# Four passes over an 8192x8192 matrix: the first pass with seven products per block from block row 4 on, one group and one join per row

## Chip, cores and metric

The kernel runs on one core of one Trainium2 chip. The metric is the device time of one execution in microseconds (us). The kernel before takes 1793.39 us, the median of three runs (1792.01 to 1795.44).

## What is computed

The matrix `adj` (8192x8192, float32) multiplies a thin matrix of 64 features four times, each time with the result of the time before:

```python
h = relu(layernorm(x))
T1 = adj @ h
T2 = 2 * (adj @ T1) - h
T3 = 2 * (adj @ T2) - T1
x = x + h @ w[0] + T1 @ w[1] + T2 @ w[2] + T3 @ w[3] + bias0
h = relu(layernorm(x))
p = tanh(norm(h)) * h / (norm(h) + 1e-8)        # norm clipped to [0, 10]
s = adj @ p
x = x + (arctanh(norm(s)) * s / (norm(s) + 1e-8)) @ kernel + bias1   # norm clipped to 0.999
```

## The kernel before

The matrix is cut into 16x16 blocks of 512x512 (1 MB, numbers `(r, c)`: r is the rows of the result, c the rows of the thin matrix that it multiplies). A block holds four chunks of 128. Blocks come from HBM through `ring`, 13 slots of one block each, all issued by SyncE in one fixed order; a load waits on `visits_done` until the last visit of the block that had its slot is over. `nodes[:, chunk, A or B, :]` holds the thin matrices: A is h, later T2; B is T1, later p. The level of a product is 1 (from h), 2 (from T1), 3 (from T2), 4 (from p).

`work_order()` writes out one list of steps, and every engine walks through that list. The steps that TensorE runs ("visits") are:

- `FRESH(r, c)`: level 1 alone from a loaded block, into `row_bank` (L627). Eight matmuls in the hardware, of 128x512.
- `BOTH(r, c)`: two levels from one load. In the first sweep levels 1 and 2 for a block left of the diagonal, into one of three `work_bank` in turn (L638 and L640), which VectorE adds to `partial[:, r, :]` after each block (L1036; the first is a copy, L1033).
- `AGAIN(r, c, level)`: one more level from a block that is in the ring already (L757), added by VectorE (L1050 to L1056). In the first sweep this is level 2 of the diagonal block.
- `OWN`: level 3 alone.
- `H_TURN`, `H_TERM`: small products with h in row 0 (L794, L807).

After the last block of a row comes `SUM` (VectorE L1079 and ScalarE L874 put the row into `acc`), then `TURN` on TensorE (L840, into `turned`), then VectorE writes the features of the next level into `nodes` (L1155, L1157, L1197). Only then may a visit use them (`s_known`).

There are three sweeps over the matrix. The first gives level 1, and level 2 for blocks on and left of the diagonal; the second, backwards, gives level 2 right of the diagonal together with level 3; the third the rest of level 3 with level 4. In the first sweep before the change `rows` (FRESH, row by row) and `columns` (one AGAIN, then BOTH down a column) are two queues, and the loop takes one of each in turn, a BOTH as soon as level 2 of its column is known. It ends with the corner of rows and columns 13 to 15.

In the second and third sweep some rows are "fast" (`is_fast`): TensorE makes seven half-size products per block in place of eight (L689). For this VectorE first forms three differences of block parts ("mixing", L1021, L1025, L1027, into `ring` slots that are given up, double-buffered by `mix_of`), two visits ahead of the visit, and GpSimd forms four sums of features (L582 to L587) once per column. At the end of a fast row ScalarE copies and exchanges halves of the two banks (L884, L887), and VectorE joins them (`JOIN`, L1116 to L1135). While rows are fast, 5 of the 13 slots (`GIVEN_UP`) hold sums and mixed blocks, and 8 are left for loads. `fast` pairs of banks alternate, so that one row is joined while the next one runs. In the second sweep column 13 (`PLAIN_COLUMN`) is done without the seven products, and its block is not mixed (L709).

```python
    while rows or columns:
        if columns and (next_is_known(columns) or not rows):
            v = columns.pop(0)
            visit(*v)
            if v[0] == "AGAIN":
                continue
        if rows:
            visit(*rows.pop(0))
```

Of the kernel before, what the change touches and what calls it, by code (L numbers as in the profile page):

```python
# [7 lines left out]
FAST_BELOW, FAST_FROM, LATE_FROM = 10, 6, 8  # L8
# [3 lines left out]
def work_order():  # L12
# [49 lines left out]

    def both_columns(row):
        if sweep[0] == 0:
            return range(min(row, HIGH))
# [4 lines left out]
    def row_complete(row, level):  # L70
        both = all((sweep[0], "BOTH", row, c) in done for c in both_columns(row))
        if level == 1:
            return both and all((0, "FRESH", row, c) in done for c in range(min(row, HIGH), NB))
        if level == 2 and row >= HIGH:
            return all((0, "AGAIN", row, c) in done for c in range(HIGH, NB))
# [4 lines left out]
    def visit(kind, row, col, *level):  # L80
        steps.append((kind, row, col) + level)
        done.add((sweep[0], kind, row, col))
        if kind == "AGAIN":
# [8 lines left out]
    def next_is_known(queue):  # L92
        kind, row, col, *level = queue[0]
        if kind == "AGAIN":
            summed = ("JOIN" if row >= FAST_FROM else "SUM", row, 3)
# [3 lines left out]


# [14 lines left out]
    while rows or columns:  # L115
        if columns and (next_is_known(columns) or not rows):
            v = columns.pop(0)
            visit(*v)
            if v[0] == "AGAIN":
                continue  # L120
        if rows:
            visit(*rows.pop(0))
        if left:
            steps.append(left.pop(0))
    for c in range(HIGH, NB):
        for r in (range(HIGH, NB) if c < NB - 1 else reversed(range(HIGH, NB))):
            visit("AGAIN", r, c, 2)
# [49 lines left out]
def with_sums(steps):  # L177

    out, waiting, corner = [], [], True
    last_corner = [s for s in steps if s[0] == "AGAIN" and s[3] == 3][-1]  # L180
    for s in steps:
        out.append(s)
        if s == ("SUM", 0, 2):
            corner = True
        if s[0] == "TURN" and s[2] == 2 and s[1] >= LOW:
            waiting.append(("SUMS", s[1], 3))
        if s[0] == "EXPAND" and s[1] < NB - 2:
            waiting.append(("SUMS", s[1], 4))
        if s in (last_corner, ("AGAIN", LOW, LOW, 4)):
            corner = False  # L190
        if not corner:
# [7 lines left out]
def is_fast(row, level):  # L199

    return level == 2 and row < FAST_BELOW or level == 3 and row >= FAST_FROM
# [36 lines left out]
def chebyshev_hyperbolic_kernel(nc, x, adj_blocks, cheb_weight, cheb_bias, hyp_kernel, hyp_bias, out):  # L238
# [18 lines left out]
    bank_no, bank_users = {}, []  # L257
# [15 lines left out]
    fast = [i for i in in_order if steps[i][0] == "BOTH" and phase_of[i] > 0 and is_fast(steps[i][1], phase_of[i] + 1)]  # L273
# [3 lines left out]
    fast_rows = [s[1:] for s in steps if s[0] == "SUM" and is_fast(*s[1:])]  # L277
    fast_second = sum(level == 2 for r, level in fast_rows)
# [8 lines left out]
    last_visit_of = [0] * len(first_step_of)  # L287
    for i, s in enumerate(steps):
# [981 lines left out]
```

How the kernel before makes its waits and increments, by code:

```python
        @block.sync  # L535
        def _(sp):
            def load_x(g):
                rows = slice(H_GROUPS[g][0] * C, (H_GROUPS[g][-1] + 1) * C)
                sp.dma_start(resid[:, rows, :], x[:, rows, :]).then_inc(s_x[g], 16)
            for n in range(loads):
                r, c = steps[first_step_of[n]][1:3]
                if n == 0:
                    load_x(0)
                    load_x(1)
                if n + 2 < len(H_GROUPS):
                    load_x(n + 2)
                if freed_by[n]:
                    sp.wait_ge(s_visit, freed_by[n])
                sp.dma_start(ring[:, slot_of[n], :, :], adj_blocks[(r * NB + c) * P:(r * NB + c + 1) * P, :, :])\
                    .then_inc(s_landed[slot_of[n]], 16)
            for s in steps:
                if s[0] == "RESULT":
                    for r in s[1:]:
                        if r in by_pool:
                            sp.wait_ge(s_pooled, by_pool.index(r) + 1)
                        else:
                            sp.wait_ge(s_result, by_vector.index(r) + 1)
                        sp.dma_start(out[:, chunks(r), :], resid[:, chunks(r), :]).then_inc(s_out, 16)
            sp.wait_ge(s_out, NB * 16)
# [1 line left out]
        @block.gpsimd  # L562
# [1 line left out]
            nc.gpsimd.memset(ident[:, :], 0.0)  # L564
            nc.gpsimd.memset(w_h[:, :, :], 0.0).then_inc(s_zeroed, 1)
            pool.wait_ge(s_zeroed, 1)
            nc.gpsimd.affine_select(out=ident[:, :], in_=ident[:, :], compare_op=ALU.not_equal, fill=1.0,
```

## Time and profile before

| | |
|---|---|
| median of the runs | 1793.39 us |
| profiled execution, its own time | 1793.74 us |
| its span, first to last instruction | 1791.8 us |
| granted TensorE clock | 0.997 |
| TensorE busy | 1756.5 us (98%) |
| VectorE busy | 962.0 us (54%) |
| loads of blocks | 626, 660.64 MB on the load queue |
| HBM read | 658.74 MB |
| start of the second sweep's first BOTH | 726.75 us |

The span leaves out what lies before the first and behind the last instruction (1.9 us here). Busy shares are means over three sweeps, which differ; the rows below are therefore taken by stretch. A line like L689 stands for one source line of the kernel before.

### The profile page before, as it was taken

What the parts mean: (1) busy time and instruction counts of PE and PEld (TensorE: products, weight loads), DVE (VectorE), ACT (ScalarE), POOL (GpSimd) and SP (SyncE); (2) the same over time, 40 slices, a digit from 0 to 9 for tenths busy, and PEclk for the clock granted to TensorE, in tenths of its full rate; (3) what the DMA queues carried; (4) which work ended last, traced back from release to release, by engine and by line L of the source; (5) the groups of instructions that cost most, each with busy time, mean ns of one, the idle gap of its engine ahead of it and who ended that gap; (6) DMA issues with size and microseconds to landing.
All of it is one profiled execution on the core that took longest, in us unless ns stands there. A gap on an engine that the chain in (4) does not pass through costs nothing.

```text
span 1791.8 us, 44489 instructions
## 1 busy us (share of the span) xinstructions
PE 1756.5 (98%) x20100; PEld 889.1 (50%) x20100; DVE 962.0 (54%) x1540; ACT 177.1 (10%) x333; POOL 126.4 (7%) x173
## 2 busy tenths in 40 slices
PE   7999999999999999999999999999999999999997
PEld 4544444444444444456666654345554454544443
DVE  7211211112111223268888886558788877876856
ACT  1000000000000000011011001311111111010014
POOL 0000000000000000221100100211001100110003
PEclk9999999999999999999999999999999999999998
DMA  9999999999999994689999988599999999999995
GB/s 370 421 422 420 422 421 413 397 397 389 377 388 383 388 361 185 251 312 330 330 339 341 334 321 339 223 348 384 417 419 419 420 419 411 419 410 418 419 420 217
DMA packets 94923, 663.72 MB, mean 370 GB/s; under 512 B 11408, under 2 KB 13712, under 8 KB 14608
## 3 DMA queue, kind: packets, MB, share of 16 engines
q1 hardware_dynamic: 93744, 660.64, 93.0%
q8 instruction: 160, 2.62, 0.6%
q10 hardware_dynamic: 992, 0.23, 0.1%
q14 instruction: 27, 0.22, 0.0%
HBM read 658.74 MB, written 2.10 MB: 369 GB/s over the span
## 4 chain that ended last, share of the span: by engine, by line
PE 87%; DVE 6%; DMA 5%; issue 1%; SPq 1%; ACT 0%; DVEq 0%
PE work_bank L638 19%; PE work_bank L757 14%; PE own_bank L689 13%; PE row_bank L689 13%; PE row_bank L627 13%; DMA ring<-adj_blocks 5%; PE row_bank L734 4%; PE work_bank L640 3%; PE turned L840 2%; DVE ring L1021 1%; PE own_bank L782 1%; PE work_bank L709 1%; PE work_bank L782 1%; DVE ring L1025 1%; DVE partial L1056 1%
## 5 line engine op out<-in xcount | busy, mean ns | idle before, releaser
L638 PE MATMUL work_bank<-ring,nodes 128*64 128x512 f32 x936 | 420.8, 592 | 0.0
L640 PE MATMUL work_bank<-ring,nodes 128*64 128x512 f32 x936 | 420.8, 592 | 0.0
L757 PE MATMUL work_bank<-ring,nodes 128*32 128x512 f32 (+1 forms) x2600 | 327.9, 593 | 8.8 <-DVE nodes L1197 4.8
L1036 DVE TENSOR_TENSOR partial<-partial,work_bank 128x512 f32<-128x512 f32 x102 | 70.1, 687 | 405.0 <-PE work_bank L640 405.0
L627 PE MATMUL row_bank<-ring,nodes 128*64 128x512 f32 x1112 | 269.8, 595 | 8.1 <-DMA ring<-adj_blocks 8.1
L689 PE MATMUL row_bank<-ring 128*32 128x256 f32 x3104 | 267.7, 379 | 0.2
L689 PE MATMUL own_bank<-ring 128*32 128x256 f32 x3104 | 267.4, 379 | 0.1
L1021 DVE TENSOR_TENSOR ring<-ring 128x1024 f32<-128x1024 f32 x194 | 238.8, 1231 | 36.8 <-PE own_bank L689 18.0
L689 PE MATMUL own_bank<-ring,nodes 128*32 128x256 f32 x2328 | 237.5, 379 | 1.3 <-DVE ring L1021 1.3
L689 PE MATMUL row_bank<-ring,nodes 128*32 128x256 f32 x2328 | 235.8, 379 | 0.7 <-DVE ring L1021 0.6
L638 PEld LDWEIGHTS work_bank<-ring,nodes 128*64 128x64 f32 x936 | 127.9, 137 | 218.0 <-issue 218.0
L757 PEld LDWEIGHTS work_bank<-ring,nodes 128*32 128x32 f32 (+1 forms) x2600 | 100.1, 112 | 160.7 <-issue 140.4
L689 PEld LDWEIGHTS row_bank<-ring 128*32 128x32 f32 x3104 | 147.4, 110 | 62.9 <-DVE ring L1025 1.6
L689 PEld LDWEIGHTS own_bank<-ring 128*32 128x32 f32 x3104 | 146.1, 110 | 63.8 <-DVE ring L1025 0.5
L627 PEld LDWEIGHTS row_bank<-ring,nodes 128*64 128x64 f32 x1112 | 104.1, 138 | 128.4 <-issue 122.4
L1056 DVE TENSOR_TENSOR partial<-partial,work_bank 128x512 f32<-128x512 f32 x141 | 96.4, 685 | 116.6 <-PE work_bank L757 115.3
L689 PEld LDWEIGHTS own_bank<-ring,nodes 128*32 128x32 f32 x2328 | 120.0, 110 | 70.0 <-issue 27.9
L689 PEld LDWEIGHTS row_bank<-ring,nodes 128*32 128x32 f32 x2328 | 121.3, 110 | 64.1 <-issue 22.4
L1025 DVE TENSOR_TENSOR ring<-ring 128x512 f32<-128x512 f32 x194 | 140.9, 726 | 6.7
L1027 DVE TENSOR_TENSOR ring<-ring 128x512 f32<-128x512 f32 x194 | 138.7, 715 | 6.6
L640 PEld LDWEIGHTS work_bank<-ring,nodes 128*64 128x64 f32 x936 | 127.9, 137 | 0.0
L574 POOL TENSOR_TENSOR resid<-resid,bias 128x256 f32<-128x256 f32 x16 | 16.8, 1050 | 854.9 <-DVE resid L1167 854.9
(148 smaller groups left out, 1004.0 us busy)
## 6 DMA issues: line engine op xcount, KB each, us to landing
ring<-adj_blocks SPq DMA_DIRECT2D x626, 1024.0 KB, 9.3
out<-resid SPq DMA_DIRECT2D x16, 128.0 KB, 1.9
resid<-x SPq DMA_DIRECT2D x7, 256.0 KB, 12.3
resid<-x SPq DMA_DIRECT2D x2, 128.0 KB, 4.3
w_raw<-cheb_weight ACTq DMA_DIRECT2D x2, 64.0 KB, 8.7
bias<-cheb_bias ACTq DMA_DIRECT2D x1, 32.0 KB, 4.1
bias<-hyp_bias ACTq DMA_DIRECT2D x1, 32.0 KB, 4.8
w_raw<-hyp_kernel ACTq DMA_DIRECT2D x2, 16.0 KB, 9.5
```

Of the source, the lines that this page charges most:

```text
L627: done = nc.tensor.matmul(bank[half, :], nodes[:, c * C + k, A, :], data[:, k, :], start=first and k < 2, stop=last and k >= 2)
L638: nc.tensor.matmul(bank[ODD, :], nodes[:, c * C + k, A, :], data[:, k, :], start=k == 0, stop=k == C - 1)
L640: done = nc.tensor.matmul(bank[EVEN, :], nodes[:, c * C + k, B, :], data[:, k, :], start=k == 0, stop=k == C - 1)
L689: done = nc.tensor.matmul(bank[lane:lane + H, columns], left(a, h, level), right[b][:, h, :], start=first and k < 2, stop=k == 6, tile_pos ...
L734: done = nc.tensor.matmul(bank[lane:lane + size, :], nodes[:, c * C + k, lane // F, lane % F:lane % F + size], data[:, k, :], start=first ...
L757: done = nc.tensor.matmul(bank[lane:lane + size, :], nodes[:, c * C + k, A if level == 3 else B, part:part + size], data[:, k, :], start=k ...
L782: done = nc.tensor.matmul(bank[lane:lane + H, :], nodes[:, c * C + k, A, part * H:(part + 1) * H], data[:, k, :], start=first and k < 2, s ...
L1021: nc.vector.tensor_tensor(first_two(n, block), block[:, :, N2].rearrange("p (k h) n -> p k h n", k=2), block[:, 0:2, :].rearrange("p h (k ...
L1025: nc.vector.tensor_tensor(mix_of(n, 1), block[:, 2:4, N2], mix_of(n, 0), ALU.subtract).then_inc(s_mixed, 1)
L1027: nc.vector.tensor_tensor(mix_of(n, 2), block[:, 2:4, N1], mix_of(n, 1), ALU.subtract).then_inc(s_mixed, 1)
L1036: nc.vector.tensor_tensor(partial[:, r, :], partial[:, r, :], bank[:, :], ALU.add)\
L1056: nc.vector.tensor_tensor(partial[:, r, :], partial[:, r, :], bank[:, :], ALU.add)\
```

## The change

In the first sweep the blocks left of the diagonal are taken row by row instead of column by column. From row 4 (`PANEL`) on they are visited with seven products; all such blocks of a row are one group: they add up in one pair of banks (`work_bank` 1 and 2, or the two `own_bank`, in turn) and are joined once (`SWAP` on ScalarE, `JOIN` on VectorE), in place of an addition to `partial` after each block. FRESH and AGAIN stay single products; from the first fast block on their matmuls, and those of TURN, are 32 columns wide and twice as many. The order between FRESH and BOTH follows a table of goals. The 5 slots are given up from the end of row 2 on, instead of from the start of the second sweep. The corner shrinks from rows 13 to 15 to rows 14 and 15 (two blocks more are BOTH, two fewer FRESH, and level 2 has two AGAIN fewer). The sums of features for level 2 are made in the first sweep. All 626 loads remain. The core of the diff:

```diff
-FAST_BELOW, FAST_FROM, LATE_FROM = 10, 6, 8
+PANEL, FAST_BELOW, FAST_FROM, LATE_FROM = 4, 10, 6, 8
...
+    def fresh_columns(row):
+        return [*range(row + 1, NB), row] if row < NB - 1 else [NB - 2, NB - 1]
...
         if sweep[0] == 0:
-            return range(min(row, HIGH))
+            return range(min(row, NB - 2))
...
+        if kind == "BOTH" and (row, col) in group_ends and sweep[0] == 0:
+            n = group_ends[row, col]
+            steps.append(("SWAP", row, 1, n))
+            follow(2, ("JOIN", row, 1, n), lambda: row_complete(row, 1) and complete(row, 1))
...
-    rows = [("FRESH", k, j) for k in range(1, HIGH) for j in [*range(k + 1, NB), k]]
-    rows += [("FRESH", k, j) for k in range(HIGH, NB) for j in range(HIGH, NB)]
-    columns = [v for k in range(HIGH) for v in [("AGAIN", k, k, 2)] + [("BOTH", r, k) for r in range(k + 1, NB)]]
...
+    rows = [("FRESH", k, j) for k in range(1, NB) for j in fresh_columns(k)]
+    blocks = [("BOTH", k, c) for k, cols, n in groups for c in cols]
+    again = [("AGAIN", k, k, 2) for k in range(NB - 2)]
...
+    goals = [(0, 0)]
+    for k in range(1, NB - 1):
+        uses = [n for n, b in enumerate(blocks) if b[2] == k]
+        goals.append((max(uses[0] - 4, goals[-1][0]) if uses else len(blocks) - 3, goals[-1][1] + NB - k))
+    both_done = fresh_done = 0
+    while rows or blocks:
+        (b0, f0), (b1, f1) = next((g for g in zip(goals, goals[1:]) if g[1][0] > both_done), (goals[-2], goals[-1]))
+        due = f0 + (f1 - f0) * (both_done + 1 - b0) / (b1 - b0)
+        may_fresh = rows and (rows[0][1] < 2 or ("SUM", rows[0][1] - 2, 1) in steps) and             (rows[0][1] < NB - 1 or not blocks)
+        may_both = blocks and next_is_known(blocks) and (blocks[0][1] < PANEL or ("SUMS", blocks[0][2]) in known)
+        if again and next_is_known(again) and ("SUMS", again[0][1]) in known:
+            visit(*again.pop(0))
+        elif may_both and (fresh_done >= due or not may_fresh):
+            visit(*blocks.pop(0))
+            both_done += 1
+        elif may_fresh:
+            visit(*rows.pop(0))
+            fresh_done += 1
...
-    return level == 2 and row < FAST_BELOW or level == 3 and row >= FAST_FROM
+    return level == 1 and row >= PANEL or level == 2 and row < FAST_BELOW or level == 3 and row >= FAST_FROM
...
+    given_up_for = [(room_from, max(visit_no[i] for i in fast if phase_of[i] == 1)), (sums_from[4], visit_no[fast[-1]])]
...
+        pairs = [[work_banks[1:], own_banks][n % 2] for n in range(groups_first)]
...
                     for k in range(C):
-                        half = (ODD, EVEN)[k % 2]
-                        done = nc.tensor.matmul(bank[half, :], nodes[:, c * C + k, A, :], data[:, k, :],
-                                                start=first and k < 2, stop=last and k >= 2)
+                        for part in range(0, F, size):
+                            lane = k % 2 * F + part
+                            done = nc.tensor.matmul(bank[lane:lane + size, :], nodes[:, c * C + k, A, part:part + size],
+                                                    data[:, k, :], start=first and k < 2, stop=last and k >= 2,
+                                                    tile_position=(0, lane))
```

Where instructions moved. On TensorE, from the end of row 0 (`turned` is the TURN of row 0, `row_bank` FRESH, `work_bank<-ring` AGAIN and BOTH, `work_bank<-w_h` and `own_bank<-ident` H_TERM and H_TURN). Before:

```order
L840 MATMUL turned<-turn,acc 64x128 x8
L807 MATMUL work_bank<-w_h,aside 64x64 x8
L757 MATMUL work_bank<-ring,nodes 64x512 x4
L638 MATMUL work_bank<-ring,nodes 64x512
L640 MATMUL work_bank<-ring,nodes 64x512
```

(the last two rows come four times, then comes one FRESH, `L627` x4, then the next BOTH, and so on in turn). Some rows behind the same TURN after the change (L692 is FRESH, L814 AGAIN, L703 the first matmul of a BOTH, L859 H_TERM, L847 H_TURN):

```order
L847 MATMUL own_bank<-ident,nodes 64x128 x4
L814 MATMUL work_bank<-ring,nodes 64x512 x4
L859 MATMUL work_bank<-w_h,aside 64x64 x8
L692 MATMUL row_bank<-ring,nodes 64x512 x4
L859 MATMUL work_bank<-w_h,aside 64x64 x8
L692 MATMUL row_bank<-ring,nodes 64x512 x96
L703 MATMUL work_bank<-ring,nodes 64x512
```

A BOTH no longer stands between each two FRESH: 24 FRESH (96 matmuls as written, four each) follow one another, to the end of row 2.

On VectorE, one row in the middle of the first sweep. Before (L1036 adds the bank of a BOTH, L1079 is SUM, L1155 and L1167 are the features after TURN, L1050 and L1051 AGAIN):

```order
L1036 TENSOR_TENSOR partial<-partial,work_bank 128x512 x10
L1079 TENSOR_TENSOR acc<-partial,row_bank 64x512
L1036 TENSOR_TENSOR partial<-partial,work_bank 128x512
L1155 COPY nodes<-turned 128x4x64
L1167 TENSOR_TENSOR resid<-resid,turned 128x256
L1050 COPY partial<-work_bank 64x512
L1051 TENSOR_TENSOR partial<-partial,work_bank 64x512
```

After, around the join of row 13 (L1072, L1076 and L1078 mix a block, L1168 to L1183 join):

```order
L1072 TENSOR_TENSOR ring<-ring 128x2x2x256
L1076 TENSOR_TENSOR ring<-ring 128x2x256
L1078 TENSOR_TENSOR ring<-ring 128x512
L1168 TENSOR_TENSOR common<-common,own_bank 128x256
L1169 SCALAR_TENSOR_TENSOR joined<-common,second_half,own_bank 128x256
L1177 TENSOR_TENSOR joined<-common,aside 128x256
L1178 TENSOR_TENSOR common<-own_bank,aside 128x256
L1183 TENSOR_TENSOR partial<-joined,common 128x512
L1072 TENSOR_TENSOR ring<-ring 128x2x2x256
L1076 TENSOR_TENSOR ring<-ring 128x2x256
L1078 TENSOR_TENSOR ring<-ring 128x512
```

One addition per block has become three mixing instructions per block and five joining ones per row, and the next mixing stands in the queue behind the join.

At the end of the first sweep on TensorE, before (L840 is TURN, L627 FRESH, L757 AGAIN, L734 the first BOTH of the second sweep):

```order
L840 MATMUL turned<-turn,acc 64x128 x8
L627 MATMUL row_bank<-ring,nodes 64x512 x16
L840 MATMUL turned<-turn,acc 64x128 x8
L627 MATMUL row_bank<-ring,nodes 64x512 x8
L757 MATMUL work_bank<-ring,nodes 64x512 x4
L840 MATMUL turned<-turn,acc 64x128 x8
L757 MATMUL work_bank<-ring,nodes 64x512 x28
L840 MATMUL turned<-turn,partial 64x128 x8
L757 MATMUL work_bank<-ring,nodes 64x512 x4
L840 MATMUL turned<-turn,partial 64x128 x8
L734 MATMUL row_bank<-ring,nodes 64x512 x8
```

and after (L759 is the end of the last fast block, L891 TURN):

```order
L759 MATMUL own_bank<-ring,nodes 32x256 x2
L692 MATMUL row_bank<-ring,nodes 32x512 x16
L814 MATMUL work_bank<-ring,nodes 32x512 x16
L891 MATMUL turned<-turn,acc 32x128 x16
L814 MATMUL work_bank<-ring,nodes 32x512 x24
L891 MATMUL turned<-turn,partial 32x128 x16
```

The corner's visits have become fewer: two FRESH and five AGAIN between the last fast block and the TURN that opens level 3, where before six FRESH and eight AGAIN stood.

## Rows read from the trace of the kernel before

**Rows 1.** Page, part 1: busy time by engine
```profile
PE 1756.5 (98%) x20100; PEld 889.1 (50%) x20100; DVE 962.0 (54%) x1540; ACT 177.1 (10%) x333; POOL 126.4 (7%) x173
```

**Rows 2.** Chain of waits, 135 to 300 us: start, length, what
```profile
143.07 1.72 PE work_bank L757 x8
...
148.22 1.72 PE row_bank L627 x8
...
153.37 1.72 PE row_bank L627 x8
...
215.17 0.88 PE turned L840 x16
...
217.76 1.72 PE work_bank L757 x8
```

**Rows 3.** Timeline of TensorE: first AGAIN, first BOTH of the second sweep
```profile
60.68 1.94 PE L757 MATMUL work_bank<-ring,nodes 128*64 128x512 f32 x8
...
726.75 3.65 PE L734 MATMUL row_bank<-ring,nodes 128*64 128x512 f32 x16
```

**Rows 4.** SyncE's waits before loads, 60 to 700 us: total, times, longest
```profile
SPq L550 <- PE work_bank L640: 381.6, 116, 4.8
SPq L550 <- PE row_bank L627: 146.8, 100, 2.2
```

**Rows 5.** Windows: PE, PEld, DVE, ACT, POOL busy, clock, DMA share, GB/s
```profile
0.00:50.00 50.00, 39.07 (x373) 22.95 (x375) 36.15 (x81) 6.80 (x22) 0.85 (x7) 1.00 0.95 376
50.00:100.00 50.00, 49.95 (x365) 24.20 (x361) 9.82 (x18) 2.65 (x7) 0.00 (x0) 1.00 1.01 420
100.00:150.00 50.00, 50.00 (x248) 23.16 (x246) 9.04 (x15) 0.59 (x1) 0.00 (x0) 1.00 1.01 421
150.00:200.00 50.00, 50.00 (x236) 22.63 (x234) 6.45 (x10) 0.00 (x0) 0.00 (x0) 1.00 1.01 421
200.00:250.00 50.00, 50.00 (x248) 23.17 (x246) 9.43 (x15) 0.59 (x1) 0.00 (x0) 1.00 1.01 422
```

**Rows 6.** Chain of waits in the fast parts, second and third sweep
```profile
948.38 27.20 PE own_bank L689 x504
...
1273.36 3.02 PE row_bank L689 x56
1276.38 1.72 PE work_bank L757 x16
```

**Rows 7.** Windows as in Rows 5, second sweep and third sweep
```profile
900.00:1000.00 100.00, 100.00 (x1907) 61.25 (x1900) 88.31 (x114) 11.16 (x20) 11.96 (x15) 1.00 0.92 337
1550.00:1650.00 100.00, 98.01 (x1492) 49.50 (x1488) 70.02 (x101) 8.18 (x15) 5.13 (x5) 1.00 1.01 414
```

**Rows 8.** Timeline of TensorE in row 0, with idle time before
```profile
17.61 1.94 PE L627 MATMUL row_bank<-ring,nodes 128*64 128x512 f32 x8 [1.10 <-DMA ring<-adj_blocks]
...
31.60 1.94 PE L627 MATMUL row_bank<-ring,nodes 128*64 128x512 f32 x8 [1.32 <-DMA ring<-adj_blocks]
```

**Rows 9.** Timeline around a join: ScalarE's exchange, mixing, VectorE's join
```profile
843.52 1.23 DVE L1021 TENSOR_TENSOR ring<-ring 128x1024 f32<-128x1024 f32 x1 [0.34 <-PE own_bank L689]
843.58 0.38 ACT L884 ACTIVATE common<-own_bank 128x256 f32<-128x256 f32 x1 [18.85 <-PE own_bank L689]
...
845.50 0.69 DVE L1027 TENSOR_TENSOR ring<-ring 128x512 f32<-128x512 f32 x1
...
848.32 0.69 DVE L1128 TENSOR_TENSOR joined<-joined,common 128x512 f32<-128x512 f32 x1
```

**Rows 10.** Block loads issued from 740, 900, 1100 and 1250 us on, to landing
```profile
ring<-adj_blocks SPq DMA_DIRECT2D x5, 1024.0 KB, 4.8
...
ring<-adj_blocks SPq DMA_DIRECT2D x32, 1024.0 KB, 5.6
...
ring<-adj_blocks SPq DMA_DIRECT2D x10, 1024.0 KB, 7.4
...
ring<-adj_blocks SPq DMA_DIRECT2D x179, 1024.0 KB, 11.6
```

More of the change, by code:

```diff
@@ L41, in known_now @@
             known.add((level + 1, row))
+            if level == 1:
+                follow(3, None, lambda: known.add(("SUMS", row)))
         def norm():
@@ L72, in row_complete @@
         if level == 1:
-            return both and all((0, "FRESH", row, c) in done for c in range(min(row, HIGH), NB))
+            joined = all(g in steps for g in joins_of.get(row, []))
+            return both and joined and all((0, "FRESH", row, c) in done for c in fresh_columns(row))
         if level == 2 and row >= HIGH:
-            return all((0, "AGAIN", row, c) in done for c in range(HIGH, NB))
+            return all((0, "AGAIN", row, c) in done for c in range(min(row, NB - 2), NB))
         if level == 4:
@@ L82, in visit @@
         done.add((sweep[0], kind, row, col))
+        if kind == "BOTH" and (row, col) in group_ends and sweep[0] == 0:
+            n = group_ends[row, col]
+            steps.append(("SWAP", row, 1, n))
+            follow(2, ("JOIN", row, 1, n), lambda: row_complete(row, 1) and complete(row, 1))
+        elif kind == "BOTH" and sweep[0] > 0 and is_fast(row, sweep[0] + 1):
+            if all((sweep[0], "BOTH", row, c) in done for c in both_columns(row)):
+                steps.append(("SWAP", row, sweep[0] + 1, 0))
         if kind == "AGAIN":
@@ L94, in next_is_known @@
         if kind == "AGAIN":
-            summed = ("JOIN" if row >= FAST_FROM else "SUM", row, 3)
+            summed = ("JOIN", row, 3, 0) if row >= FAST_FROM else ("SUM", row, 3)
             return (level[0], col) in known and (level[0] < 4 or summed in steps)
         return (2 + sweep[0], col) in known
+    groups = [(k, range(min(k, NB - 2)), 0) for k in range(1, NB)]
+    group_ends = {(k, cols[-1]): n for k, cols, n in groups if k >= PANEL}
+    joins_of = {}
+    for k, cols, n in groups:
+        if k >= PANEL:
+            joins_of.setdefault(k, []).append(("JOIN", k, 1, n))
     steps += [("H", g) for g in range(3)]
@@ L122, in work_order @@
             visit(*rows.pop(0))
+            fresh_done += 1
+        else:
+            visit(*blocks.pop(0))
+            both_done += 1
         if left:
             steps.append(left.pop(0))
-    for c in range(HIGH, NB):
-        for r in (range(HIGH, NB) if c < NB - 1 else reversed(range(HIGH, NB))):
-            visit("AGAIN", r, c, 2)
+    for r, c in [(NB - 2, NB - 2), (NB - 3, NB - 2), (NB - 1, NB - 2)] + [(r, NB - 1) for r in reversed(range(HIGH, NB))]:
+        visit("AGAIN", r, c, 2)
@@ L177, in with_sums @@
 def with_sums(steps):
-    out, waiting, corner = [], [], True
-    last_corner = [s for s in steps if s[0] == "AGAIN" and s[3] == 3][-1]
+    out, waiting, room = [], [], False
     for s in steps:
@@ L183, in with_sums @@
         if s == ("SUM", 0, 2):
-            corner = True
-        if s[0] == "TURN" and s[2] == 2 and s[1] >= LOW:
-            waiting.append(("SUMS", s[1], 3))
+            room = False
+        if s[0] == "TURN" and (s[2] == 1 and s[1] < NB - 2 or s[2] == 2 and s[1] >= LOW):
+            waiting.append(("SUMS", s[1], s[2] + 1))
         if s[0] == "EXPAND" and s[1] < NB - 2:
             waiting.append(("SUMS", s[1], 4))
-        if s in (last_corner, ("AGAIN", LOW, LOW, 4)):
-            corner = False
-        if not corner:
+        if s in (("SUM", PANEL - 2, 1), ("AGAIN", LOW, LOW, 4)):
+            room = True
+        if room:
             out += waiting
```

263 lines of the change are left out of this document (142 added, 121 removed).

## Prediction

> **What bounds the kernel now.** The page's busy shares come first: TensorE is busy 98% of the span [rows 1], so every other engine matters only where TensorE waits for it. The shares mix three sweeps, so the chain of waits of the first sweep is next. There FRESH takes 1.72 us and the next FRESH begins 5.15 us later, which leaves 3.43 us for the BOTH between; TURN takes 0.88, AGAIN 1.72 [rows 2]. From one AGAIN at 143.07 to the next at 217.76 there is 1.72 + 14 x 5.15 + 0.88 = 74.7 us of work in 74.69 us of time, so TensorE has no gap. The same sum over the stretch from the first AGAIN at 60.68 to the second sweep's first BOTH at 726.75 [rows 3]: 122 FRESH (209.8), 117 BOTH (401.3), 22 AGAIN (37.8), 17 TURN (15.0) make 663.9 us, and 666.07 are measured; the 2.2 between are the five H_TURN and H_TERM that lie there too, 0.44 each. The first sweep is TensorE's time and nothing else, and these prices can be trusted to a microsecond.
>
> How far away is the next limit? The windows show the loads at 420 to 422 GB/s from 50 to 250 us [rows 5], which is 2.49 us for a block of 1.05 MB. TensorE takes two blocks in 5.15 us, the loads need 4.98. SyncE's waits before loads are for TensorE's visits, 528 us of them [rows 4]: the ring is full and the loads are paced by TensorE. But the spare is 3% only. That is what decides this change: it makes TensorE faster where the loads have almost nothing left to give.
>
> **What the change removes and adds, on TensorE.** A fast visit costs 27.20 / 9 = 3.02 us (504 matmuls are nine blocks), and in the third sweep it costs the same between single products: 1273.36 to 1276.38, then AGAIN 1.72 [rows 6]. So a BOTH gets 0.41 us cheaper. There are 113 fast ones (rows 4 to 13 have as many as their number, rows 14 and 15 have 14 each) and six old ones. FRESH goes from 139 to 137, AGAIN from 22 to 20. Before: 239.1 + 401.3 + 37.8 = 678.2 us. After: 235.6 + 20.6 + 341.3 + 34.4 = 631.9. TensorE's work falls by 46.3 us. Matmuls of 32 columns, twice as many, cost what the wider ones do: AGAIN is 1.72 as 8 of them and as 16 [rows 2, 6].
>
> **What of it the loads allow.** The order is now by rows. Row k (from 4 on) is 16 - k FRESH, k fast BOTH, one AGAIN and one TURN: (16 - k) x 1.72 + k x 3.02 + 2.60 = 30.1 + 1.30 k us. Its 16 loads need 39.8. These are equal at k = 7.5. Rows up to 7 are therefore bound by the loads, with TensorE starved, and rows from 8 on by TensorE. In rows 1 and 2 it is plainest: 24 FRESH of 1.72 us follow one another while a block comes every 2.49 us. Formerly BOTH of late rows filled this time; now they come late, where the loads could be faster than TensorE and nobody needs it.
>
> So the end is found at the place where starving stops: the first FRESH after row 7's third BOTH, block (7, 9). By the order of the steps it is the 117th load (92 FRESH and 24 BOTH stand ahead in the load order). The eighth block was waited for and begun at 31.60 us [rows 8], so it landed at about 31.5, and row 0 is unchanged; 109 more at 2.49 land at 31.5 + 271.4 = 302.9 us. Behind it TensorE has 45 FRESH (77.4), 96 fast BOTH (289.9), 14 AGAIN (24.1) and 11 TURN (9.6), 401.0 us in all, until the second sweep's first BOTH. That gives 703.9 us. Block (6, 6) or block (8, 9) as the turning point gives the same within 1 us, as two nearly equal rates must.
>
> **What must be added to it.** (1) Eight slots instead of 13 from the end of row 2 on. The trace has loads at the limit with eight slots only in the third sweep, between 1250 and 1650 us: 414 GB/s in the lowest of these windows [rows 7], 2.53 us a block. For the 55 loads concerned that is 0 to 2.4 us; I take 1. (2) Mixing: from 843.52 to 846.19 on VectorE [rows 9], 2.67 us a block, against 3.02 on TensorE. In the second sweep VectorE is 88% busy and TensorE 100% [rows 7], so it is covered. But a join stands in front of the next mixing. ScalarE's exchange begins at 843.58, the join's last instruction ends at 849.01 [rows 9], 5.4 us after the group. Where FRESH stand between the blocks (1.72 us of spare each) this is hidden. Behind rows 13 and 14 two fast visits are mixed late: the mixing that follows the join ends its first part some 0.4 us after TensorE wants it. (3) TURN of row 4 comes after two FRESH and a BOTH, 6.5 us after its group; exchange and join need 5.4, what SUM adds is estimated at 1.4 from two instructions like the join's last (0.69 each) as an upper end, 6.1 to 6.8 in all. The same holds for row 15. Together (2) and (3) are 0.5 to 4 us; I take 1.5. (4) The last row: the four corner blocks already loaded stay in the ring, so four slots stream 11 blocks of 3.02 us. A slot's turn is landing, one visit of mixing and one visit: landing may take 6.04 us. Loads alone land in 4.8, in the second sweep in 5.6 [rows 10], so 0; at 7.4, as from 1100 us on, it would be 1.36 / 4 = 0.34 us a block, 3.7 in all. (5) The features' sums on GpSimd, begun at the end of row 2, have the 12 visits between TURN and the block that needs them. The joined totals go straight to `partial`, and 117 additions vanish from VectorE, which costs and wins nothing, for they were waits of VectorE for TensorE.
>
> Sum: 703.9 + 1 + 1.5 = 706.4 against 726.75, 20.3 us earlier. The second and third sweep keep their visits and their ring; there TensorE is busy 98 to 100% [rows 7] and nothing in it starts later. The profiled execution took 1793.74 us (its span 1791.8 and 1.9 around it), so 1773.4; it lies 0.35 above the median of the runs, so the forecast for the median is **1773 us**. Less than half of TensorE's saving arrives, the other 26 us go to waiting for blocks.
>
> **The rivals.**
> *The ring runs short.* With eight slots, one in the visit, two held for mixing and one by the diagonal block, four are in flight. If landing takes 11.6 us as in the third sweep [rows 10], that is 2.90 us a block. If only while the diagonal block waits (5 of 17 visits), 55 x 0.41 x 5/17 = 6.6 us; if always, 22.6 and the gain is gone. For it: no stretch before has this holding at full rate with seven products. Against it: the 11.6 us are mostly queueing, and a load alone lands in 4.8, so two in flight are enough. Time about 1780 to 1796, likeliest 1783.
>
> *The handover between rows.* Each group must be joined, summed, turned and written before the next row's last block. If each of 12 rows loses 1 to 1.5 us, it is 12 to 18 us: 1785 to 1791. For it: the first sweep has no plain column that gives VectorE 3.4 us for the join. Against it: five to ten visits lie between join and need.
>
> *The clock falls (slower).* Through rows 1 and 2 TensorE works 1.72 of 2.49 us, 69%. If the granted clock fell to 1.2 GHz there, FRESH would take 3.44 us, 0.95 more than the loads' pace. The gain of 20.3 us is used up by 22 such FRESH; the 24 in a row and the 13 of row 3 would cost 35 us, 1808 us; with just the 24, 1796. Against it: in row 0 TensorE waits 1.10 and 1.32 us before FRESH [rows 8], its busy time is 39 of 50 us, and the granted clock is 1.00 [rows 5].
>
> The Trainium skill (TensorE: Matmul & The Clock Gate, Part 1: The HAM clock gate) says that the chip passes half of the clock when it has seen TensorE little busy; by that rule the starved rows are where this change would pay, and the trace of row 0 does not bear it out.
>
> *The loads do not bind.* Then all of 46.3 us arrive, 1747. A block every 1.72 us would be 610 GB/s; no window shows more than 422. *All is bound by the loads*: the 256th block lands at 31.5 + 248 x 2.49 = 649 us, long before 706, so this can't be.
>
> **How the numbers follow.** Forecast 0.70, own range 1768 to 1780 (no additions: 1770.6; with 2.4, 4 and 3.7: 1778). Ring short 0.11, handover 0.08, clock 0.06, better than 1767 0.02, no change for some other reason 0.03. Range 1767 to 1787: it takes in most of the second and a part of the third. Within 0.2% (3.6 us) is what these runs can't tell from no change. Faster takes the forecast, nearly all of the ring and most of the handover: 0.89. Same 0.03. Slower is the clock and the ring at its worst: 0.08.
>
> **What would show it.** In the windows from 60 to 280 us TensorE busy falls to some 70 to 95%, its waits before FRESH name the load of the ring, about 26 us in all more than now, at 415 to 421 GB/s and clock 1.00. From 310 to 700 us it is 99 to 100% busy, with loads falling to about 350 GB/s. The second sweep's first BOTH begins at 704 to 710. The rest keeps its length. The prediction is wrong if idle time is found behind 350 us (handover), if GB/s lies below 410 while TensorE waits for loads (ring), if the clock row is below 1.00, or if the later sweeps change their length.

## The result, and the profile after

| | before | after |
|---|---|---|
| median, us | 1793.64 (1792.01 to 1795.44, 4 runs) | 1775.76 (1775.46 to 1775.99, 4 runs) |
| profiled execution, its span, us | 1793.74, 1791.8 | 1775.57, 1773.5 |
| second sweep's first BOTH, us | 726.75 | 711.19 |

The ratio is 0.99 with a 95% interval of 0.9883 to 0.9917: the changed kernel is 17.9 us faster, where 20 were forecast.

The page of the kernel after, parts 1 and 2: busy time by engine, then TensorE's share and the traffic in 40 slices of 44.3 us.

```profile
PE 1719.4 (97%) x25836; PEld 947.7 (53%) x25836; DVE 1207.1 (68%) x1826; ACT 209.9 (12%) x393; POOL 163.3 (9%) x229
PE   7979999999999999999999999999999999999997
GB/s 373 420 422 421 421 419 420 420 407 404 402 381 371 316 327 315 294 321 332 335 341 328 341 325 307 251 356 391 419 419 419 419 420 411 418 410 416 419 419 237
```

TensorE is busy 37.1 us less than in [rows 1], yet the profiled execution is only 18.2 us shorter: the other 18.9 are idle time that was not there before. The traffic row shows the second half of the forecast: some 420 GB/s to slice 8, then a fall from 407 in slice 9 to 315 in slice 16, the last one that lies in the first sweep.

The windows of the kernel after (columns as in [rows 5]) say where TensorE is idle.

```profile
50.00:100.00 50.00, 44.34 (x324) 18.61 (x320) 4.47 (x10) 3.10 (x7) 0.00 (x0) 1.00 1.01 421
100.00:150.00 50.00, 41.75 (x196) 12.70 (x194) 4.19 (x7) 0.59 (x1) 0.00 (x0) 1.00 1.01 421
150.00:200.00 50.00, 48.84 (x326) 19.27 (x326) 12.70 (x19) 0.59 (x1) 7.05 (x16) 1.00 1.01 421
200.00:250.00 50.00, 46.25 (x644) 20.10 (x640) 22.65 (x30) 3.34 (x6) 3.44 (x4) 1.00 1.01 420
250.00:300.00 50.00, 48.04 (x688) 21.28 (x684) 28.21 (x40) 6.07 (x11) 1.79 (x4) 1.00 1.01 419
...
350.00:400.00 50.00, 48.75 (x756) 24.87 (x752) 31.54 (x40) 3.33 (x6) 4.25 (x6) 1.00 1.00 407
...
600.00:650.00 50.00, 50.00 (x900) 30.01 (x895) 41.75 (x53) 3.58 (x7) 3.06 (x4) 1.00 0.87 314
...
900.00:1000.00 100.00, 100.00 (x1892) 73.06 (x1887) 87.39 (x109) 7.27 (x13) 11.71 (x15) 1.00 0.92 338
```

Where [rows 5] have 49.95 or 50.00 of 50, TensorE now works 41.75 to 48.84 up to 300 us, with the loads at 419 to 421 GB/s and the granted clock at 1.00. Behind 400 us it is full again and the loads fall below what they can do. The second sweep reads as in [rows 7].

TensorE's waits from 60 to 720 us in the kernel after: who waits for whom, total, times, longest.

```profile
PEld row_bank L692 <- DMA ring<-adj_blocks: 50.3, 44, 2.3
...
PE row_bank L692 <- DMA ring<-adj_blocks: 18.0, 30, 1.4
...
PE row_bank L692 <- DVE acc L1130: 1.6, 1, 1.6
...
PE turned L891 <- issue: 1.3, 2, 0.9
...
PE work_bank L703 <- DMA ring<-adj_blocks: 0.8, 2, 0.6
```

18.8 of the some 22 us of the PE rows are waits for the load of a block; the PEld row counts 44 weight loads that waited for one. The timeline shows their rhythm in row 1, with the idle time before each in brackets, and then the two waits of a TURN and the end of the sweep.

```profile
73.74 1.94 PE L692 MATMUL row_bank<-ring,nodes 128*64 128x512 f32 x8 [0.19 <-DMA ring<-adj_blocks]
76.22 1.94 PE L692 MATMUL row_bank<-ring,nodes 128*64 128x512 f32 x8 [0.54 <-DMA ring<-adj_blocks]
78.70 1.94 PE L692 MATMUL row_bank<-ring,nodes 128*64 128x512 f32 x8 [0.55 <-DMA ring<-adj_blocks]
...
389.66 1.08 PE L891 MATMUL turned<-turn,acc 128*32 128x128 f32 x32 [0.95 <-issue]
...
663.75 1.08 PE L891 MATMUL turned<-turn,acc 128*32 128x128 f32 x32 [0.32 <-issue]
...
711.19 3.64 PE L799 MATMUL row_bank<-ring,nodes 128*32 128x512 f32 x32
```

A FRESH begins every 2.48 us, the loads' pace, though its work is 1.72. In [rows 3] the last of these lines stood at 726.75: 15.56 us are won here. The remaining 2.6 us come behind it. The chain of waits of the kernel after, for block (7, 9), which the forecast rests on, and for the end of the third sweep:

```profile
291.69 15.38 DMA ring<-adj_blocks
307.11 1.92 PE row_bank L692 x16
309.04 3.02 PE own_bank L759 x56
...
1697.99 3.43 PE work_bank L835 x32
1701.43 5.15 PE work_bank L814 x48
1706.58 0.31 issue
```

The chain of the kernel before at the second of these places:

```profile
1714.35 3.43 PE work_bank L782 x32
1717.78 5.15 PE work_bank L757 x48
1722.93 2.30 issue
```

1714.35 - 1697.99 is 16.36, so 0.8 us were won in small pieces between the second sweep's start and here, and 2.30 - 0.31 = 2.0 in this one gap before an AGAIN. The profile calls the gap "issue", but the timeline shows what ends it. Before:

```profile
1718.53 0.38 ACT L884 ACTIVATE common<-own_bank 128x256 f32<-128x256 f32 x1
...
1721.46 0.43 DVE L1125 TENSOR_TENSOR joined<-common,aside 128x256 f32<-128x256 f32 x1 [1.49 <-ACT aside L887]
...
1724.44 0.69 DVE L1051 TENSOR_TENSOR partial<-partial,work_bank 64x512 f32<-64x512 f32 x1
...
1725.23 1.92 PE L757 MATMUL work_bank<-ring,nodes 128*32 128x512 f32 x16 [2.30 <-issue]
```

After:

```profile
1698.12 0.38 ACT L935 ACTIVATE common<-own_bank 128x256 f32<-128x256 f32 x1 [39.11 <-PE own_bank L759]
...
1706.10 0.69 DVE L1102 TENSOR_TENSOR partial<-partial,work_bank 64x512 f32<-64x512 f32 x1
...
1706.89 1.92 PE L814 MATMUL work_bank<-ring,nodes 128*32 128x512 f32 x16 [0.31 <-issue]
```

In both kernels the AGAIN begins 0.10 us after VectorE has added a `work_bank` to `partial`, and this addition stands behind the join of row 15. Before, the join waited for ScalarE's exchange, 0.44 and 1.49 us, because the exchange was part of SUM and came 4.2 us after the row's last fast block. The change makes it a step of its own (`SWAP`) directly behind that block, in the later sweeps too:

```diff
+        elif kind == "BOTH" and sweep[0] > 0 and is_fast(row, sweep[0] + 1):
+            if all((sweep[0], "BOTH", row, c) in done for c in both_columns(row)):
+                steps.append(("SWAP", row, sweep[0] + 1, 0))
```

So these 2.0 us belong to a second part of the change, which has nothing to do with the order of the first sweep. The gap is 2.30 in the two kernels without this step (the kernel before, and the same with eight slots) and 0.31 in all others of this study. No run moved the step by itself; the cause is read from the timelines.

### The profile page after: what moved, and what is told of

Same layout as the page of the kernel before. It is cut to its first block, busy times and chain, and to the rows that moved or that the text cites. A ratio compares the mean times of both kernels' runs of the same rounds, so it can differ in the third digit from the quotient of the medians.

```text
span 1773.5 us, 56434 instructions
## 1 busy us (share of the span) xinstructions
PE 1719.4 (97%) x25836; PEld 947.7 (53%) x25836; DVE 1207.1 (68%) x1826; ACT 209.9 (12%) x393; POOL 163.3 (9%) x229
## 4 chain that ended last, share of the span: by engine, by line
PE 78%; DMA 13%; DVE 7%; issue 1%; ACTq 0%; ACT 0%; DVEq 0%
PE own_bank L759 23%; PE work_bank L814 14%; PE row_bank L759 13%; DMA ring<-adj_blocks 13%; PE work_bank L759 8%; PE row_bank L692 8%; PE row_bank L799 4%; PE turned L891 2%; DVE ring L1072 1%; PE own_bank L835 1%; PE work_bank L775 1%; PE work_bank L703 1%; DVE ring L1076 1%; PE work_bank L835 1%; DVE partial L1107 1%
## 5 line engine op out<-in xcount | busy, mean ns | idle before, releaser
L1072 DVE TENSOR_TENSOR ring<-ring 128x1024 f32<-128x1024 f32 x307 | 378.6, 1233 | 129.1 <-PE own_bank L759 44.0
L759 PE MATMUL own_bank<-ring 128*32 128x256 f32 x4992 | 430.7, 379 | 0.1
L759 PE MATMUL own_bank<-ring,nodes 128*32 128x256 f32 x3744 | 383.0, 379 | 1.2 <-DVE ring L1072 1.2
L814 PE MATMUL work_bank<-ring,nodes 128*32 128x512 f32 (+1 forms) x2744 | 324.3, 593 | 6.7 <-DVE nodes L1265 4.8
L759 PEld LDWEIGHTS own_bank<-ring 128*32 128x32 f32 x4992 | 255.3, 110 | 86.2 <-DVE ring L1076 0.5
L692 PE MATMUL row_bank<-ring,nodes 128*32 128x512 f32 (+1 forms) x1688 | 262.2, 597 | 26.9 <-DMA ring<-adj_blocks 24.4
L759 PE MATMUL row_bank<-ring 128*32 128x256 f32 x3104 | 268.4, 379 | 0.2
L759 PEld LDWEIGHTS own_bank<-ring,nodes 128*32 128x32 f32 x3744 | 209.1, 110 | 99.5 <-issue 45.2
L759 PE MATMUL row_bank<-ring,nodes 128*32 128x256 f32 x2328 | 236.7, 379 | 0.7 <-DVE ring L1072 0.6
L1076 DVE TENSOR_TENSOR ring<-ring 128x512 f32<-128x512 f32 x307 | 220.2, 717 | 10.5
L1078 DVE TENSOR_TENSOR ring<-ring 128x512 f32<-128x512 f32 x307 | 218.1, 710 | 10.5
L759 PEld LDWEIGHTS row_bank<-ring 128*32 128x32 f32 x3104 | 160.1, 110 | 52.7 <-DVE ring L1076 1.6
L814 PEld LDWEIGHTS work_bank<-ring,nodes 128*32 128x32 f32 (+1 forms) x2744 | 95.5, 110 | 156.2 <-issue 135.5
L759 PEld LDWEIGHTS row_bank<-ring,nodes 128*32 128x32 f32 x2328 | 131.4, 110 | 56.8 <-issue 22.3
L692 PEld LDWEIGHTS row_bank<-ring,nodes 128*32 128x32 f32 (+1 forms) x1688 | 76.0, 118 | 158.8 <-issue 94.1
L759 PE MATMUL work_bank<-ring 128*32 128x256 f32 x1728 | 148.9, 379 | 0.0
L759 PE MATMUL work_bank<-ring,nodes 128*32 128x256 f32 x1296 | 132.7, 379 | 0.0
L759 PEld LDWEIGHTS work_bank<-ring 128*32 128x32 f32 x1728 | 86.1, 110 | 31.6
L759 PEld LDWEIGHTS work_bank<-ring,nodes 128*32 128x32 f32 x1296 | 70.5, 110 | 36.9 <-issue 18.2
```

The costliest lines, as they stand in the source:

```text
L692: done = nc.tensor.matmul(bank[lane:lane + size, :], nodes[:, c * C + k, A, part:part + size], data[:, k, :], start=first and k < 2, stop= ...
L759: done = nc.tensor.matmul(bank[lane:lane + H, columns], left(a, h, level), right[b][:, h, :], start=first and k < 2, stop=k == 6, tile_pos ...
L814: done = nc.tensor.matmul(bank[lane:lane + size, :], nodes[:, c * C + k, A if level == 3 else B, part:part + size], data[:, k, :], start=k ...
L1072: nc.vector.tensor_tensor(first_two(n, block), block[:, :, N2].rearrange("p (k h) n -> p k h n", k=2), block[:, 0:2, :].rearrange("p h (k ...
L1076: nc.vector.tensor_tensor(mix_of(n, 1), block[:, 2:4, N2], mix_of(n, 0), ALU.subtract).then_inc(s_mixed, 1)
L1078: nc.vector.tensor_tensor(mix_of(n, 2), block[:, 2:4, N1], mix_of(n, 1), ALU.subtract).then_inc(s_mixed, 1)
```

## The experiments

Each edit is to the changed kernel if nothing else is said. A time is the median of four executions, of ten for the kernel before with eight slots, and a single execution for the one with half loads. "First BOTH" is the second sweep's first BOTH in the profile of the run: 726.75 us before, 711.19 after.

### How many fast blocks are worth something

**Fast blocks from row 6 on.** Rows 4 and 5 lose their nine fast blocks, which are 3.7 us of TensorE's work, in rows where the forecast has the loads as the bound. The same line keeps the 13 slots until the end of row 4.

```diff
-PANEL, FAST_BELOW, FAST_FROM, LATE_FROM = 4, 10, 6, 8
+PANEL, FAST_BELOW, FAST_FROM, LATE_FROM = 6, 10, 6, 8
```

> Seven products only from row 6 on: rows 4 and 5 (9 blocks) are visited with eight products, 3.43 us in place of 3.02, and the ring keeps 13 slots until the end of row 4. Theory (the first sweep waits for loads until row 8): no change, the second sweep's first BOTH at 711 +- 1 us, 1776 +- 1 in all. Rival (each fast block brings 0.41 us): 3.7 us later, 1779.5. Rival (eight slots cost load rate in rows 3 to 8): 1 to 2 us earlier.

Measured: 1775.23 us (ratio to before 0.9899, 0.9884 to 0.9913), first BOTH at 710.50. Nine fast blocks are worth nothing here.

**Fast blocks from row 8 on.** The same line with `PANEL` 8: 22 fast blocks fewer, 9.0 us of work.

> Seven products only from row 8 on: 22 blocks of rows 4 to 7 at 3.43 us. Theory: loads bind until about block (5,4), the 95th load, landed at 251.8 us, and 457.9 us of TensorE's work lie behind it, so the turning point moves up and the sweep ends 1.6 us later than with the change: first BOTH of the second sweep at 712 to 713, 1777.4 in all. Rival (each fast block brings 0.41 us): 9.0 us later, 1784.8. Rival (handover between rows costs 1 us a row): 3 us earlier than the theory, for four joins fewer.

Measured: 1774.6 us (0.9895, 0.9878 to 0.9911), first BOTH at 709.82. Had each block brought its 0.41 us, this would be near 1785. The second sweep begins 1.4 us earlier than in the changed kernel, not 1.6 later as the sum of loads and work said. Its windows show that TensorE is full from 200 us on and the loads do not slacken:

```profile
200.00:300.00 100.00, 99.85 (x490) 40.59 (x488) 15.95 (x25) 1.18 (x2) 0.00 (x0) 1.00 1.01 421
300.00:400.00 100.00, 100.00 (x1194) 47.12 (x1194) 51.18 (x68) 4.51 (x8) 17.42 (x36) 1.00 1.01 416
```

Thirteen slots to the end of row 6 keep 421 GB/s where the changed kernel had 419 to 420 with eight, and there are four joins fewer.

In the starved rows this run shows something that the changed kernel does not. One block came late in row 2, and the clock fell behind the wait; in the run before (fast blocks from row 6 on) a wait of the same length at the same place, after the same waits of 0.55 us, left the clock at 1.00. First that run, then this one:

```profile
106.90 1.94 PE L692 MATMUL row_bank<-ring,nodes 128*64 128x512 f32 x8 [2.11 <-DMA ring<-adj_blocks]
```

```profile
106.82 7.07 PE L692 MATMUL row_bank<-ring,nodes 128*64 128x512 f32 x24 [2.03 <-DMA ring<-adj_blocks]
```

Three FRESH in 7.07 us are 1.7 more than at full clock; in windows of 1 us from 107 on the granted clock is 0.57, 0.50, 0.50 and 0.72, then 1.00 again (0.50 is 1.2 GHz). The loss is made up at once, as the loads are the bound there.

**Fast blocks in the last rows alone.** `PANEL` 14: 28 fast blocks, but the order by rows is kept. This prices the order by itself.

> The order by rows with seven products only in rows 14 and 15 (28 blocks in place of 113). Theory: the order alone costs, since rows 1 to 5 wait for loads and late rows pay 3.43 us a block. Turning point at load 95 (block (5,4), landed at 251.8 us) and 484 us of work behind it: first BOTH of the second sweep at 735.7, 24.5 us later than with the change and 9 later than before; 1800 in all. Rival (the order costs nothing, the gain was 113 fast blocks less stalls): at most 722, 1787. Rival (every fast block is worth 0.41 us whatever the row): 85 x 0.41 = 35 us later than the change, 1811.

Measured: 1801.37 us, ratio 1.0046 (1.003 to 1.0063), first BOTH at 736.63. With most of the seven products taken away, the new order makes the kernel slower than before: 24 FRESH stand in a row with nothing beside them, and TensorE starves there.

### Are the loads what the early rows wait for?

**Half of the data in rows 1 to 3.** The FRESH blocks of these rows are loaded by half, so that a load takes half the time; TensorE's work is unchanged. The kernel leaves out the other half of these blocks and multiplies what stood in the slot before.

```diff
+            half_loaded = {load_no[i] for i in first_step_of if steps[i][0] == "FRESH" and 1 <= steps[i][1] <= 3}
...
-                sp.dma_start(ring[:, slot_of[n], :, :], adj_blocks[...])
+                part = slice(0, 2) if n in half_loaded else slice(0, C)
+                sp.dma_start(ring[:, slot_of[n], part, :], adj_blocks[... part, :])
```

> The change, with the FRESH blocks of rows 1 to 3 loaded by half (chunks 0 and 1 only; the other half of the slot keeps what was there). All products are made. 42 loads take 1.25 us less each, 52 us in all. Theory: TensorE no longer waits for blocks, and the sweep is its work alone: TURN of row 0 at 57.7 us plus 620.6 us of work is 678.3, with some 3 us of waits at joins 681, 30 us earlier than the change; 1746 in all. Rival (the missing gain went to joins and handovers): less than 10 us earlier, 1766 or more. Rival (the clock): granted clock below 1.00 somewhere in the first sweep with full loads and higher here.

Measured, one run: 1753.53 us, first BOTH at 687.87. That is 23.3 us earlier, where 30 were expected; had the joins and TURNs been what rows wait for, nothing of the kind would have come. The windows tell where the missing 7 us are.

```profile
60.00:190.00 130.00, 128.43 (x860) 55.47 (x860) 24.11 (x37) 2.54 (x5) 7.04 (x16) 1.00 0.86 325
190.00:350.00 160.00, 157.77 (x2304) 72.68 (x2300) 91.80 (x122) 13.32 (x24) 10.44 (x16) 1.00 1.01 419
```

Up to 190 us the loads need only 325 GB/s: they could run ahead, but eight slots leave them nowhere to put the blocks. So rows 4 to 7, whose loads are whole, are at 419 GB/s with TensorE held to their pace. By the prediction's own sum a row k up to 7 is 39.8 - (30.1 + 1.30 k) us short: 4.5, 3.2, 1.9 and 0.6, 10.2 in all. This run stands 9.6 above TensorE's bare work (678.3); 1.6 of them are one wait for a row's sum and 1.1 two waits before TURN, so about 7 are left for blocks.

**The kernel before with eight slots.** The first sweep of the kernel before is given eight slots instead of 13, for its rows 2 to 11.

```diff
+    shared_from[0] = visit_no[[i for i in in_order if i < steps.index(("SUM", 2, 1))][-1]]
+    shared_to[0] = visit_no[[i for i in in_order if i < steps.index(("SUM", 11, 1))][-1]]
...
-        for level in (3, 4):
+        for level in (0, 3, 4):
```

> The kernel before, with 5 of the 13 slots unused from the end of row 2 to the end of row 11 of the first sweep. Nothing else changes. Theory (eight slots are enough, two loads in flight fill the queue): no change, within 1 us of before, 1793.6. Rival (eight slots cannot keep the loads near the limit): loads fall below 400 GB/s while TensorE waits for them, 5 to 20 us slower.

Measured: 1794.06 us, ratio 1.0001 (0.9991 to 1.001), 10 runs. Eight slots hold the loads at TensorE's pace of one block in 2.58 us.

### What the early rows could be given to do

**Three columns early, fast blocks from row 8 on.** If the loads leave TensorE idle in rows 1 to 7, old BOTH visits belong there: they make both products from one load, 3.43 us of work for a block that is loaded in 2.49, where FRESH has 1.72. The blocks of columns 0 to 2 are visited column by column as in the kernel before, with eight products, and only the rest by rows.

```diff
-PANEL, FAST_BELOW, FAST_FROM, LATE_FROM = 4, 10, 6, 8
+PANEL, EARLY, FAST_BELOW, FAST_FROM, LATE_FROM = 8, 3, 10, 6, 8
...
-    groups = [(k, range(min(k, NB - 2)), 0) for k in range(1, NB)]
+    groups = [(k, range(EARLY, min(k, NB - 2)), 0) for k in range(EARLY + 1, NB)]
...
-    blocks = [("BOTH", k, c) for k, cols, n in groups for c in cols]
+    blocks = [("BOTH", k, c) for c in range(EARLY) for k in range(c + 1, NB)]
+    blocks += [("BOTH", k, c) for k, cols, n in groups for c in cols]
```

> Columns 0 to 2 of all rows are visited early, column by column beside the FRESH of rows 1 to 3, with eight products; the other blocks row by row, in groups with seven products from row 8 on (67 fast blocks). Theory: the starved rows get work, so the sweep ends at the larger of TensorE's work (697.3) and the loads (698.2), 13 us earlier than the change with 46 fewer fast blocks: 1763 in all, 1765 with stalls. Rival (fewer fast blocks lose, 46 x 0.41): 19 us slower than the change, 1795. Rival (waits at joins and handovers keep the loss): no change, 1776.

Measured: 1769.7 us (0.9869, 0.9854 to 0.9884), first BOTH at 704.97. With 67 fast blocks instead of 113 it is 6 us faster than the change, and 4.9 us faster than the version with fast blocks from row 8 on, from which only the early columns (and the 24 fast blocks that they replace) tell it apart. The second sweep begins 7 us later than expected, and the waits name something new; from 60 to 720 us there are only these two.

```profile
PE turned L893 <- issue: 4.2, 3, 1.7
PE row_bank L694 <- DVE acc L1132: 1.6, 1, 1.6
```

No wait for a load is left. TensorE now waits for the handover: the TURN of a row comes before its joined sum is written.

**Four columns early, fast blocks from row 6 on** and **three columns early, fast blocks from row 4 on.** `EARLY` 4 with `PANEL` 6 has 64 fast blocks, `EARLY` 3 with `PANEL` 4 has 77 and drops to eight slots at the end of row 2.

> As the three-column kernel with four columns early and groups from row 6 on (64 fast blocks). Theory: TensorE's work alone, 698.6, with loads never binding behind row 0: first BOTH of the second sweep at 699 to 700, TensorE without waits for loads after 70 us, 1764 in all. Same rivals: 1796 or 1776.

> Three columns early, groups from row 4 on (77 fast blocks), eight slots from the end of row 2. Theory: TensorE's work would end at 693.2, but rows 4 to 8 are starved again (17 us short by the rows' sums) and loads bind until block (8,10), the 155th load: 698.3; the ten fast blocks more than in the row-8 kernel bring nothing, 1763 to 1766. Rival (the ring's stock of landed blocks covers the shortage): 694, 1759.

Measured: 1776.94 us (0.9906, 0.9891 to 0.9921), first BOTH at 712.14, and 1776.63 us (0.9905, 0.9891 to 0.992), first BOTH at 712.15. Both expectations failed by 11 to 14 us. In the first, the windows around the end of row 4 show a hole:

```profile
310.00:340.00 30.00, 30.00 (x154) 14.21 (x152) 4.86 (x8) 0.59 (x1) 8.75 (x20) 1.00 0.79 302
340.00:380.00 40.00, 39.09 (x182) 16.59 (x180) 3.44 (x5) 0.59 (x1) 0.00 (x0) 1.00 1.01 417
380.00:450.00 70.00, 67.35 (x794) 28.33 (x794) 36.38 (x52) 6.66 (x12) 8.66 (x12) 1.00 1.01 420
```

When five slots are given up at the end of row 4, the loads fall to 302 GB/s for 30 us, as if they stood until blocks were consumed; then TensorE is idle for 3.6 us, 1.8 of them for loads that run at 417 to 420 again and 1.6 for VectorE's sum of a row. Another 1.2 us for a block follow at 461 us, and the waits before TURN come to 5.9 us. Against the three early columns with fast blocks from row 8 on, the sweep is 7.2 us longer: 1.3 are more work, 4.8 more waits, and the rest is not assigned. In the second there are 5.2 us of those and 4.7 of waits for loads, and something more. Its windows of TensorE alone (busy, granted clock, DMA share, GB/s):

```profile
324.00:326.00 2.00, 2.00 (x12) 1.00 1.05 438
326.00:328.00 2.00, 0.44 (x3) 1.00 0.97 401
328.00:330.00 2.00, 0.79 (x2) 0.72 1.04 434
330.00:332.00 2.00, 2.00 (x8) 0.50 0.98 410
332.00:334.00 2.00, 2.00 (x32) 0.93 1.03 422
...
340.00:342.00 2.00, 0.04 (x4) 1.00 0.98 406
342.00:344.00 2.00, 2.00 (x13) 0.63 1.02 426
344.00:346.00 2.00, 2.00 (x16) 0.51 0.34 135
```

TensorE waited 2.77 us for a load, and the FRESH behind it took 3.44 us, twice its 1.72, at a granted clock of 0.50 (1.2 GHz); after 3.12 us of waiting for VectorE's `acc` the same followed.

**TURN one visit later.** The waits of TURN were tested by themselves, on the changed kernel and on the version with three columns early and fast blocks from row 8 on.

```diff
         if level == 1 and row == NB - 1:
             visits_to_turn = 3
+        elif level == 1 and row >= PANEL:
+            visits_to_turn = 4
```

> The change, with TURN of rows 4 to 14 four visits after SUM in place of two. Theory (TensorE waits 0.95 and 0.32 us at two TURNs for the sum, the rest of the missing gain is waiting for loads): at most 1.3 us earlier, 1774.5 to 1776. Rival (handover between rows is the larger part of the loss): 5 us or more earlier, 1771.

> The kernel with three columns early and groups from row 8, with TURN of rows 8 to 14 four visits after SUM. Its trace showed no wait for loads, but 4.2 us of TensorE idle before three TURNs. Theory (with loads no longer the bound, the handover is what is left): these vanish, 4 us earlier, 1765.5 to 1767. Rival (the waits move on to the AGAIN or BOTH that needs the row's features): no change, 1769.5 to 1770.5.

Measured on the change: 1773.89 us (0.9894, 0.988 to 0.9909), first BOTH at 710.01, 1.2 us earlier, and no wait of TURN is left. Measured on the other: 1766.33 us (0.9853, 0.9836 to 0.9869), first BOTH at 701.04, 3.9 us earlier, with these waits from 40 to 705 us:

```profile
PE row_bank L696 <- DVE acc L1134: 1.6, 1, 1.6
PE own_bank L763 <- DVE ring L1076: 0.4, 1, 0.4
```

This is the fastest version of the study: 1.5% below the kernel before, and some 9 us below the change.

## Why the prediction was right

The forecast was 1773 us and 1775.8 were measured, by the mechanism that was named. Point by point:

- **Saving on TensorE, 46.3 us: consistent with the page, though it shows 37.1.** A fast block is 3.02 us in the chain after (309.04), as forecast. But a FRESH that begins after a wait stands at 1.94 us in the timeline, where one in a row costs 1.72: 0.22 us more, for the 44 waits of the PEld row, is 9.7, and 46.3 - 37.1 is 9.2. Up to the second sweep's first BOTH, 46.3 - 15.6 = 30.7 us of the saving were lost, where 26 were forecast.
- **Rows up to 7 bound by loads: right, shown.** The turning block (7, 9) comes behind row 7's second BOTH, not its third; the counts of the sum are those of the right place. TensorE waits for blocks up to there, at 419 to 421 GB/s; nine and 22 fast blocks fewer in these rows cost nothing; halving the loads of rows 1 to 3 brings 23.3 us.
- **117th block landed at 302.9 plus 1: 3.2 us too early.** It landed at 307.07. The 24th block came at 73.7 where the pace from the eighth says 71.3, a term that the sum left out: 2.4 us. From 31.5 to 73.7 us the block queue moved 17.65 MB, and sixteen blocks are 16.8; the loads of `x`, which stand in the same queue, are the likely rest. The other 93 took 233.4 us, 2.51 each, 1.8 us more than at 2.49. Some 0.5 us of this may be the larger program, whose instructions are fetched on the same DMA engines (0.3% of their time before, 0.5% after, from 74 to 307 us).
- **401.0 us of work behind it plus 1.5: 404.1 measured.** 1.3 are two waits of TURN (0.95 in row 8, 0.32 in row 14), which moving TURN returned (1.2). The prediction had the size, but named rows 4 and 15 for TURN and late mixing behind rows 13 and 14, and none of these appears among TensorE's waits. The other 1.8 lie before 389 us, in small waits where two nearly equal rates meet (one of 0.28 for a block at 378.80): the end is then later than the larger of the two sums. From row 8's TURN at 389.66 on, the work is 320.8 us and the next sweep begins 321.5 later.
- **Eight slots, 1 us: not measured by itself.** It can be no more than the 1.8 us of the 93 loads above. The kernel before showed no cost at its own pace; the version with thirteen slots to row 6 gained 1.4 us together with fewer joins, and the two were not parted.
- **Last row on four slots, 0: right.** The six loads issued between 680 and 700 us landed in 5.4 us, under the 6.04 allowed.
- **Later sweeps unchanged: wrong by 2.6 us.** The prediction said that nothing in them starts later, and did not ask what starts earlier: the exchange on ScalarE does, and brings 2.0 us in the one gap. This happens to hide half of the 4.8 us by which the first sweep was missed, so that the whole looks better than its parts; that much of the 1773 is luck.
- **The signs.** The first BOTH at 711.19 lies just outside the 704 to 710 that were given for it, and two of the four signs of being wrong appeared in small: 1.3 us of waits for TURN behind 350 us, and later sweeps 2.6 us shorter.
- **The range.** With additions of 2.4, 4 and 3.7 us the forecast comes to 1780.6, not the 1778 that stands in it.

Of the rivals, *the ring runs short* did not decide: 419 GB/s and more while TensorE waited, up to 350 us. *The handover* was there with 1.3 us, not 12 to 18 (and with 1.6 us before a FRESH at 133.73, inside the starved rows, where the loads decide the end anyway); it became the next limit (4.2 us) once the loads had room. *The clock falls* did not happen in the change: waits of 0.5 to 1.4 us, up to 1.6 once, left it at 1.00. Its mechanism is real, though. It showed in the version with three columns early and fast blocks from row 4 on, after waits of 2.77 and 3.12 us, and in the starved rows themselves after 2.03 us (fast blocks from row 8 on), where it cost 1.7 us of TensorE and nothing of the sweep. A single late block was enough. The Trainium skill (TensorE: Matmul & The Clock Gate, Part 1: The HAM clock gate) has the chip at half clock once TensorE sat idle; the traces agree where TensorE waited for 2.03, 2.77 and 3.12 us, not where it waited for 2.11, and the starved rows of the change, 41.75 busy of 50 us in waits of half a microsecond, are no such place. *The loads do not bind* is excluded by the half loads.

Open stay the 0.8 us in small pieces of the later sweeps, why one block in row 2 came late in two of the versions, and how the 1.4 us between fast blocks from row 4 and from row 8 divide among slots, joins and instruction fetch.

## What to carry to other kernels

Before an engine is made faster, sum its work and the loads' time stage by stage from the place of the change on, and take the largest of "block n has landed, plus all work behind it": here this gave the end of the sweep within 5 us and said beforehand that less than half of the saving would arrive. How many units got cheaper is no measure: 67 fast blocks beat 113, because the visits with more work per load than a load takes were put beside those with less. And when one wait is cleared, read the waits again: the handover, worth 1.3 us in the change, was worth 4 behind it. Last, look at what a change moves outside the stage that it is meant for: one step placed earlier for all sweeps gave 2.0 of the 17.9 us.

## What was not expected of the hardware

- One core's loads held 419 to 421 GB/s for 250 us while TensorE waited for them in small steps: the stalls of the consumer cost the full queue nothing that the windows show.
- TensorE's granted clock stayed 1.00 with waits of 0.55 us before every 1.72 us of work (41.75 busy in 50). Behind single waits of about 2 us it went either way: 1.00 after 2.11 us in one version, 0.50 after 2.03 us in another. Behind 2.77 us it was 0.50, and behind 3.12 us it fell to 0.51.
